# A transformer stage on one core: the feed-forward's narrowing moved into the next step

## What is computed

```python
for i in range(6):                                            # DEPTH
    x = attn_layer(shift_tokens(x), Wqkv[i], q_scale[i], k_scale[i], Wo[i]) + x
    x = ffn_layer(shift_tokens(x), ln_g[i], ln_b[i], W1[i], b1[i], W2[i], b2[i]) + x

# attn_layer: qkv = x @ Wqkv; l2norm and rotary tables on q and k of 16 heads of 64;
#   softmax over the own and the previous window of 32 tokens; out @ Wo
# ffn_layer: layernorm; hg = xn @ W1 + b1 (2 x 341 wide); a, gate = split(hg)
#   return a * gelu(gate) @ W2 + b2
```

## Time and profile before

| | |
|---|---|
| median of 3 runs | 4747.47 us |
| profiled execution, its own time | 4748.92 us |
| its span | 4747.2 us |
| TensorE matmul busy | 4319.4 us (91%), 69192 matmuls |
| VectorE busy | 3144.3 us (66%) |
| ScalarE busy | 2720.9 us (57%) |
| GpSimd busy | 2628.5 us (55%) |
| transformer stage | about 210 to 3563 us of the span |

### The profile page before, as it was taken

The page is one execution under the profiler, slowest core; times in us unless marked ns, Lnnn a source line. Parts: engine busy times, 40 slices in busy tenths (PEclk is TensorE's granted clock), DMA queues, the critical chain, the costliest instruction groups (busy, mean ns, idle before and its releaser), DMA issues. The chain is left out here.

```text
span 4747.2 us, 156031 instructions
## 1 busy us (share of the span) xinstructions
PE 4319.4 (91%) x69192; PEld 2792.5 (59%) x69192; DVE 3144.3 (66%) x4110; ACT 2720.9 (57%) x3930; POOL 2628.5 (55%) x1468
## 2 busy tenths in 40 slices
PE   7489999999999999999999999999975999788868
PEld 5256666666666666666666666666652554344435
DVE  4477776777667776777767777777733443699974
ACT  4246666666666666666656666666642443577743
POOL 0266666666666666666666666666622112477752
PEclk8699999999999999999999999999986999899999
DMA  2111212221222112211122122211111000211110
GB/s 56 52 34 42 48 45 64 49 48 45 54 54 52 44 46 59 56 44 45 44 62 50 44 49 58 55 44 47 46 30 33 1 1 1 93 72 72 72 35 16
DMA packets 230431, 221.12 MB, mean 47 GB/s; under 512 B 137657, under 2 KB 185794, under 8 KB 227714
## 3 DMA queue, kind: packets, MB, share of 16 engines
q1 hardware_dynamic: 229761, 211.13, 17.0%
HBM read 68.50 MB, written 4.03 MB: 15 GB/s over the span
## 5 line engine op out<-in xcount | busy, mean ns | idle before, releaser
L1018 POOL TENSOR_TENSOR tf_qk<-tf_qk,tf_rot 128x1024 f32<-128x1024 f32 x384 | 909.7, 2369 | 1135.0 <-DVE tf_rot L1396 1134.3
L1084 PE MATMUL tf_psum<-tf_Wqkv,tf_xsT 128*128 128x512 f32 x1536 | 738.3, 603 | 45.3 <-issue 20.0
L1025 POOL TENSOR_TENSOR tf_qk<-tf_qk,tf_rn 128x1024 f32<-128x1024 f32 x384 | 722.6, 1903 | 63.4 <-ACT tf_rn L1277 63.4
L1270 ACT ACTIVATE tf_sq<-tf_psum 128x1024 f32<-128x1024 f32 x384 | 393.9, 1026 | 507.9 <-DVE tf_rot L1396 507.9
L1392 DVE TENSOR_TENSOR tf_qk<-tf_psum,tf_table 128x1024 f32<-128x1024 f32 x384 | 467.6, 1218 | 239.3 <-PE tf_psum L1084 235.7
L1402 DVE TENSOR_REDUCE tf_ss<-tf_sq 128x16 f32<-128x1024 f32 x384 | 457.8, 1192 | 23.4 <-ACT tf_sq L1270 23.4
L1396 DVE TENSOR_TENSOR tf_rot<-tf_psum,tf_table 128x1024 f32<-128x1024 f32 x384 | 466.4, 1215 | 0.0
L1084 PEld LDWEIGHTS tf_psum<-tf_Wqkv,tf_xsT 128*128 128x128 f32 x1536 | 271.4, 192 | 325.2 <-issue 299.3
L1066 PE MATMUL tf_psum<-ident,tf_qk 128*128 128x128 f32 x3072 | 405.5, 275 | 22.1 <-ACT tf_qT L1292 2.4
L1150 PE MATMUL tf_psum<-tf_probT,tf_Vback 64*64 64x32 f32 x12288 | 396.1, 222 | 26.6 <-DVE tf_z L1437 16.0
L1066 PEld LDWEIGHTS tf_psum<-ident,tf_qk 128*128 128x128 f32 x3072 | 344.0, 141 | 112.8 <-issue 110.6
(11 more groups left out here) (319 smaller groups left out, 7961.8 us busy)
## 6 DMA issues: line engine op xcount, KB each, us to landing
tf_Vback<-tf_V SPq DMA_DIRECT2D x384, 128.0 KB
tf_Vback<-tf_V SPq DMA_DIRECT2D x576, 64.0 KB
mb_Csb<-mb_kept SPq DMA_DIRECT2D x16, 2048.0 KB, 7.1
tf_zr<-z SPq DMA_DIRECT2D x96, 128.0 KB, 2.7
z<-tf_z SPq DMA_DIRECT2D x48, 256.0 KB, 2.5
tf_Wqkv<-in_Wqkv_split SPq DMA_DIRECT2D x18, 512.0 KB, 3.8
tf_zu<-z SPq DMA_DIRECT2D x97, 64.0 KB
tf_zu<-z SPq DMA_DIRECT2D x97, 63.5 KB
```

Source lines behind the costliest of these rows:

```text
L1018: nc.gpsimd.tensor_tensor(v, v, rot[:, kind, :], ALU.add).then_inc(added.sem, 1)
L1025: nc.gpsimd.tensor_tensor(v, v, rn[:, t, HEADS * kind:HEADS * (kind + 1)].unsqueeze(2) .to_broadcast([P, HEADS, HD]), ALU.mult).then_inc(n ...
L1084: last = nc.tensor.matmul(proj[:, half, :], xsT[:, step.unit(0), WIN + t * P:WIN + (t + 1) * P], Wqkv[:, c:c + 512], start=True, stop=True)
L1270: nc.scalar.activation(sq[:, kind, :], flat2(proj), ACT.Square).then_inc(squared.sem, 1)
```

## The change

The narrowing of pair J, and its addition, are issued one step later. TensorE does them in ff 0 of the next pair, behind `turn_probs` and ahead of the keys' projection; VectorE adds behind `centre`. A new method `past()` gives the pair whose narrowing falls into a step. In such steps the output projection and its addition stand behind the keys' projection, as they did in ff 3 (where they stay). At the end of ff 3 nothing is left behind `turn_input`. The same instructions are issued in the same number; SyncE's, GpSimd's and ScalarE's lists are unchanged.

```diff
+    def past(self):
+        J = self.pair() - 1
+        return J if self.k % 4 == 0 and 0 <= J < UNITS // 2 else None
...
             def narrow(step):
-                J = step.pair()
+                J = step.past()
                 pe.wait_ge(gated.sem, gated.at(J, 3))
-                if step.has(3):
-                    pe.wait_ge(o_copied.sem, o_copied.at(step.tile(3), 1))
-                elif step.has(4):
-                    pe.wait_ge(z_added.sem, z_added.at(step.tile(4), 1))
+                if step.has(4):
+                    pe.wait_ge(o_copied.sem, o_copied.at(step.tile(4), 1))
+                else:
+                    pe.wait_ge(z_added.sem, z_added.at(TILES - 1, 1))
...                                   (TensorE's body)
-                if step.has(4) and ff != 3:
+                if step.past() is not None:
+                    narrow(step)
+                later = ff == 3 or step.past() is not None
+                if step.has(4) and not later:
                     output(step)
                 if step.has(0):
                     project(step, 1)
-                if step.has(4) and ff == 3:
+                if step.has(4) and later:
                     output(step)
...
-                elif ff == 3:
-                    narrow(step)
...                                   (VectorE's body)
+                if step.past() is not None:
+                    add_hidden(step.past(), step.past() % 2)
+                later = ff == 3 or step.past() is not None
-                if step.has(4) and ff != 3:
+                if step.has(4) and not later:
                     add_output(step)
                 if step.has(0):
                     sum_squares(step, 0)
                     rope(step, 1)
-                if step.has(4) and ff == 3:
+                if step.has(4) and later:
                     add_output(step)
...
-                elif ff == 3:
-                    add_hidden(step.pair(), step.k // 4 % 2)
```

## The result

The change makes the kernel slower: 4861.1 us median (4858.4 to 4871.2, 4 runs) against 4745.1 us of the kernel before (4735.7 to 4749.9, 4 runs), ratio 1.0244, 95% interval 1.0227 to 1.0260. That is +116 us where 71.9 were forecast: the sign was right, the size was not, and 4861 lies above the range.

The account below looks back on a forecast made before the run. TensorE was taken as the bound between 420 and 3480 us. Lost cover of 44.1 us, 26.8 us and 0.95 us, together 71.9, on 4747.5 gave 4819.4 us, range 4803 to 4840.

Parts of the forecast that it names:

- The cover that goes, ordinary seams: From ff 3 to ff 0, the queries' projection waits uncovered for ScalarE's input copy: 1.26 us at each of 35 seams.
- Late seams: At 10 seams around layer changes SyncE's count already comes late, so the narrowing's whole 2.68 us is added each time.
- the first rival: TensorE's clock falls after waits of about 4 us at 10 seams, costing 19 us, 4838 in all; chance 0.05.
- the plain sum: The forecast's added terms over the whole kernel, with no clock fall: 71.9 us slower, 4819; chance 0.77.
- A wait that is doubled: In ff 0 attend now also waits for the output's addition behind the keys' rope: 0 to 10.8 us, taken as 0.
- TensorE's work is unchanged: The narrowing's same 24 matmuls run in the new place, 48 times, so all of the result lies in waits.
- New order within ff 0: With narrowing and output moved, the keys' rope is at most 0.08 us late and the output does not wait.
- statistics: VectorE's statistics wait for the shifted output but end 0.27 us before the rope could start: zero cost.
- SyncE: The pair's save waits for the later addition, but SyncE is busy until then and nothing queued is late: zero.
- the last seam: Behind pair 45 there is no projection, but the scores wait for the eviction of the values: 0.95 us.
- The other side: A rival: VectorE paces the seam, so the move gains 6 to 16 us, down to 4731; chance 0.03.

Follow-up runs that it names:

- e3: Changed kernel, but the 10 seams where SyncE's count comes late keep the old place of narrowing, its addition and the output; 4825.6 us.
- e4: Changed kernel, with the narrowing's 24 matmuls done once more, result unused, in the old place at the 10 seams with SyncE's late count; 4848.5 us.
- e5: Changed kernel, with the output projection of ff 0 written to the score bank, so attend no longer waits for its addition; 4823.7 us.
- e7: Changed kernel, with the narrowing's 24 matmuls done once more, result unused, in the old place at all 45 seams; 4889.2 us.
- e1: Changed kernel, with the next input's transposition and copy put ahead of the values' projection and their eviction; 4869.7 us.
- e10: Changed kernel, with the next input transposed between the halves of the values' projection in ff 3 and copied ahead of their eviction; 4849.5 us.
- e2: Kernel before, with only the output projection of ff 0 and its addition put behind the keys' projection, narrowing unmoved; 4809.1 us.
- e6: Kernel before, with the output projection of ff 3 written to the score bank, so attend waits for the third product instead; 4712.5 us.

## Why the prediction was wrong

- **The cover that goes, ordinary seams: right.** 1.26 us forecast, 1.27 (median) measured.
- **Late seams: right in kind, a little large in the cover, short of the clock.** TensorE waited 36.7 us for the count at L952, some 40 forecast, and the lost cover is 21 us, 26.8 forecast. But the clock fell at 9 of 10, about 2.2 us each (projection 3.57 for 1.82, mask 0.99 for 0.52). That was the first rival, given 0.05 and priced at 19 us; it came true beside the plain sum, not in its place. I had set it as a case of its own because the early steps kept the full clock, but their waits were 1.1 us and these 2.5 to 3.9. e3 and e4 show it: the waits filled, the clock falls at two seams instead of nine, and the groups that it lengthens lose 15.6 us.
- **"A wait that is doubled": the step that failed.** It was bounded by 0 and 10.8 us and taken as 0. The visible wait was indeed free (-3.4 us): the gap ahead of attend in ff 0 is 0.08 us at the median, too short for the list of waits. What was left out is that behind such a wait the next block of code is late. e5 measures the price at 37.4 us (31.5 against the kernel before beside it), of which its profile shows 17 in the attend that waits and 11 in the scores of the next step. The trace of before had it already: 18.7 us of "issue" in 23 places at attend, which the prediction does not mention. Over the 44 cycles 16 of the delays in attend's second half stand in ff 3, the one phase where attend waited, and 2 in all others.
- **"TensorE's work is unchanged", so all else zero: wrong for the scores of ff 0**, +11.5 us. With the 2.68 us gone from ahead of them TensorE comes sooner to the scores, 256 instructions, a whole block of code, behind the dense code of attend. e7 puts the work back and the delay goes; e1 and e10 shorten the stretch further and it grows (86.7, 85.8). Some 3 of the 11.5 us stand at the late seams, where the clock is low too (75.0 us in e3, which keeps those seams).
- **New order within ff 0, statistics, SyncE, the last seam: right** as far as the profile shows (last seam 1.03 us longer, 0.95 forecast; VectorE idle 0.27 us ahead of the rope, as worked out). The other side was never near: VectorE's 5.05 us wait was not a price TensorE paid.

Sum of the measured parts in the 44 cycles: cover 64 us (about 70 forecast for them), clock 19 (17.6 + 3.7 less 0.07 at each ordinary seam), code 33 (11.5 + 6.4 + 15.0, some 3 of it rather the clock's). So the clock and the code, both at zero in the plain sum, make up 52 us, and the cover came out 7 us smaller than forecast: together the 45 us by which the 116.4 lie above 71.9.

What stays open: why a wait at attend delays the scores a step later as well, why in e7 less of that is left though attend still waits, and how much of the code's delay is the fetch itself and how much the time at which it is asked for. The runs show when the delay appears, at which place of a block, and that it follows the packets; they don't show the sequencer. That a wait makes the next block late is inferred from the table above and from e2, e5 and e6.

## What to carry to other kernels

Where TensorE is 97% busy, look at what each group covers in other engines' chains before moving it: the narrowing was work that had to be done anyway, standing where a copy, a weight load and a code fetch needed the time. Sort the "issue" delays by place in the schedule: if they gather behind one wait, that wait can cost more than its own row says (e6: 27 us gained, where the row said 16.0; e5: 31 to 37 us, where the wait was in no row), and writing the awaited result to another bank can remove both. Counting TensorE's instructions in blocks of 256 tells such delays from others: they all stand at one place of the block. And a repeated wait of 3 to 4 us in an otherwise dense stretch has to be priced with the clock that follows it.

## What was not expected of the hardware

- Code fetch shows on TensorE at 550 packets of 16 KB: 64 delays of over 0.3 us in the changed kernel's steady stretch, each ending 1.1 to 1.7 us behind a packet and each at record 193 to 195 of a block of 256. In the kernel before, a block's edge in attend's second half was delayed 16 times in 22 behind a wait (ff 3), and without one 2 times in 21 (ff 0) and never in 39 (ff 1 and ff 2).
- At the late seams `turn_input` and the wait behind it took 2.9 to 4.4 us, in a stretch that is otherwise busy. The projection behind was at the pace of 1.2 GHz (3.49 us or more for 1.82) at 8 of the 10, in part at one (2.86) and not at all at one. Where they took 1.5 to 1.8 us it was so at none of 35.
